# A recurrence stage with four rows to a partition: seven scan matmuls in place of ten, one queue for its transfers

## What is computed

```python
kv = ctx * ctx
r  = 0.9 * r + kv_t                 # row after row
x  = x + layernorm(x) * r           # first stage
h  = relu(quant_linear(layernorm(x), w1, b1))
x  = x + quant_linear(h, w2, b2)    # second and third stage
```

## Time and profile before

| | |
|---|---|
| median of 3 runs | 1264.55 us (1264.29 to 1264.74) |
| the profiled execution: its time | 1265.31 us |
| its span | 1263.5 us |
| mean granted clock of TensorE | 0.987 of full speed |
| TensorE matmuls busy | 1213.5 us, 96% |
| ScalarE busy | 979.9 us, 78% |
| VectorE busy | 872.2 us, 69% |
| GpSimd busy | 162.3 us, 13% |
| moved by DMA | 448.78 MB |

### The profile page before, as it was taken

One profiled execution on the slowest core, in us unless ns is written; L12 is line 12 of the kernel. 1 busy time (PEld: TensorE's weight loads), 2 busy tenths in 40 slices (PEclk: granted clock), 3 DMA queues, 4 the chain that ended last, 5 costly groups with the idle time before them and its releaser, 6 DMA issues.

```text
span 1263.5 us, 15533 instructions
## 1 busy us (share of the span) xinstructions
PE 1213.5 (96%) x5386; PEld 562.1 (44%) x5386; DVE 872.2 (69%) x1262; ACT 979.9 (78%) x1211; POOL 162.3 (13%) x394
## 2 busy tenths in 40 slices
PE   5998999999699999999999999799999999999997
PEld 2444444444344444444444444344444444444443
DVE  4887999886577777777777777566545655654554
ACT  4788999887577777777777776688887888888776
POOL 2646556444000000000000000000000000000000
PEclk9999999999799999999999999899999999999999
DMA  9999999972277799999999998699999999999998
GB/s 354 403 406 333 389 363 341 346 277 81 118 321 289 305 394 407 359 365 362 362 358 351 348 363 317 229 334 419 418 417 417 417 418 417 417 418 416 416 417 325
DMA packets 134614, 448.78 MB, mean 355 GB/s; under 512 B 10740, under 2 KB 10760, under 8 KB 123400
## 3 DMA queue, kind: packets, MB, share of 16 engines
q1 hardware_dynamic: 94744, 331.40, 66.2%
q10 hardware_dynamic: 39792, 116.40, 25.8%
HBM read 254.81 MB, written 192.94 MB: 354 GB/s over the span
## 4 chain that ended last, share of the span: by engine, by line
PE 80%; POOL 6%; issue 5%; DVE 4%; DMA 3%; ACT 2%; SPq 1%; ACTq 0%; POOLq 0%; DVEq 0%
PE ps L833 35%; PE ps L875 33%; PE ps L811 9%; PE ps L855 2%; DMA xq<-hidden_scratch 2%; POOL xq L444 2%; DVE st L644 1%; DVE st L630 1%; DVE xq L639 1%; DMA xq<-in_x_dram 1%; POOL rstd L436 1%; POOL cs_bc L428 1%; ACT xq L478 1%; ACT xq L589 0%; SPq L317 0%
## 5 line engine op out<-in xcount | busy, mean ns | idle before, releaser
L875 PE MATMUL ps<-w2T,xq 128*128 128x512 f16 x2048 | 446.4, 381 | 4.2 <-ACT xq L589 3.8
L833 PE MATMUL ps<-xq,w1T 128*128 128x512 f16 x2048 | 448.7, 380 | 1.4 <-DVE xq L710 1.4
L589 ACT ACTIVATE xq<-xq,hb,hs 128x512 f16<-128x512 f32 x494 | 357.3, 801 | 83.6 <-PE ps L875 57.5
L701 DVE TENSOR_REDUCE work<-xq 128x2 f32<-128x1024 f32 x255 | 311.0, 1220 | 125.9 <-ACT xq L534 125.9
L534 ACT ACTIVATE xq<-ps 128x1024 f32<-128x1024 f32 x255 | 260.9, 1023 | 123.1 <-PE ps L833 122.9
L875 PEld LDWEIGHTS ps<-w2T,xq 128*128 128x128 f16 x2048 | 200.0, 98 | 250.6 <-ACT xq L589 9.8
L811 PE MATMUL ps<-xq,work 128*128 128x512 f32 x640 | 283.0, 603 | 24.7 <-ACT xq L468 24.7
L833 PEld LDWEIGHTS ps<-xq,w1T 128*128 128x128 f16 x2048 | 199.1, 98 | 237.0 <-issue 1.9
L749 DVE TENSOR_TENSOR work<-ps,cs_bc 128x512 f32<-128x512 f32 x128 | 88.4, 691 | 185.0 <-PE ps L875 178.6
L811 PEld LDWEIGHTS ps<-xq,work 128*128 128x128 f32 x640 | 122.9, 193 | 178.0 <-issue 161.0
L478 ACT ACTIVATE xq<-ps,ones,cs_bc 128x512 f32<-128x512 f32 x128 | 98.9, 772 | 24.8 <-PE ps L811 23.8
(11 more groups left out here) (99 smaller groups left out, 444.9 us busy)
## 6 DMA issues: line engine op xcount, KB each, us to landing
hidden_scratch<-xq SPq DMA_DIRECT2D x240, 512.0 KB, 6.0
xq<-hidden_scratch SPq DMA_DIRECT2D x232, 512.0 KB, 21.2
work<-x_scratch ACTq DMA_DIRECT2D x42, 1024.0 KB, 11.4
xq<-in_ctx_dram ACTq DMA_DIRECT2D x31, 1024.0 KB, 9.2
xq<-in_x_dram SPq DMA_DIRECT2D x24, 1024.0 KB, 12.0
x_scratch<-xq SPq DMA_DIRECT2D x24, 1024.0 KB, 8.4
out_dram<-work ACTq DMA_DIRECT2D x24, 1024.0 KB, 12.0
xq<-in_L_ffn_w_dram SPq DMA_DIRECT2D x8, 1024.0 KB, 7.8
```

What stands on the lines that cost most here:

```text
L589: act.activation(hq[c % HQ], src[:, c % 2, :], ACT.Relu, bias=hb[:, q:q + 1], scale=hs[:, q:q + 1]).then_inc(h_scaled, 1)
L701: dve.tensor_reduce(hmax[:, b * NF + 2 * q:b * NF + 2 * q + 2], src, AX.X, ALU.max).then_inc(kept_maxed, 1)
L833: last = pe.matmul(bank, w1T[:, k, f * P:(f + 1) * P], xq_rows(b, k), start=(k == 0), stop=(k == KD - 1))
L875: last = pe.matmul(acc_bank(s, i), src[:, i * P:(i + 1) * P], w2T[:, q, :], start=first, stop=final)
```

## The change

- **Rows.** Partition p holds rows 4 p to 4 p + 3 of a batch; tile i holds rows 4 p + i. The three rearranges read `(p i)`; a partition's part of a batch is now 8 KB in one piece in DRAM, before four pieces of 2 KB.
- **Scan.** Tile 0 takes four matmuls over all four tiles of squares (`scan_first`). Tiles 1 to 3 each add one matmul on the same bank: the tile's own squares times a diagonal matrix with 0.9 to the power of -i (`scan_next`). The factor 0.9 to the power of i that this leaves out is put into the reciprocal deviation of x by three new constants (`half_x`, `per_row_x`, `eps_x`). That is seven matmuls a batch. The one bank of a batch is read by ScalarE between these steps, so `scan_next` waits until ScalarE has read the tile before.
- **Order.** Tiles of batch j and j + 1 are interleaved: (j+1, 0), (j, 2), (j+1, 1), (j, 3). A ring of four tiles holds the scaled sums, before eight. ScalarE squares batch j + 3 at the end of round j.
- **Rings.** CS is 4, statistics rings 8 batches, x statistics one batch further ahead (XLEAD = 4), LEAD 6.
- **Transfers.** SyncE issues all of the first stage: in each round the store of the finished batch, x, a weight quarter, ctx. The load of ctx waits for `scan_ready` of the batch whose buffer it takes.
- **Weights.** VectorE copies one of the two turned halves (`keep_weights`, 128x1024 float16), ScalarE the other.
- **End.** The y statistics of the last two batches are one group, before two.

```diff
-            ctx_rows = ctx_in.rearrange("b (i p) d -> b p i d", p=P)
+            ctx_rows = ctx_in.rearrange("b (p i) d -> b p i d", p=P)
...
+    for j in range(-1, NB):
+        scans += [t for t in ((j + 1, 1), (j, 3), (j + 1, 2), (j + 2, 0)) if 0 <= t[0] < NB]
+        tiles += [t for t in ((j + 1, 0), (j, 2), (j + 1, 1), (j, 3)) if 0 <= t[0] < NB]
...
+            def load_ctx(j):
+                if j >= CS:
+                    sp.wait_ge(scan_ready, scan_at[(j - CS, NI - 1)] + 1)
+                sp.dma_start(ct[j % CS], ctx_rows[j]).then_inc(ctx_loaded[j % CS], 16)
...
             for j in range(NB):
+                if j > 0 and j - 1 not in late:
+                    store_x2(j - 1)
                 if j + LEAD < NB:
                     load_x(j + LEAD)
                 for m in weights_at(j + 2):
                     if m > 0:
                         load_weights(m)
-                if j > 0 and j - 1 not in late:
-                    store_x2(j - 1)
+                if j + CS < NB:
+                    load_ctx(j + CS)
...
             def factors(j, i):
-                act.wait_ge(scan_ready, u + 1)
-                wait_count(act, x2_done, u + 1 - 2 * NI)
-                act.activation(g1[j % 2][:, i, :], scan_bank(j, i), ACT.Identity, bias=ones[:, 0:1],
+                act.wait_ge(scan_ready, scan_at[(j, i)] + 1)
+                wait_count(act, x2_done, n + 1 - len(g1))
+                act.activation(g1[n % len(g1)], scan_bank(j), ACT.Identity, bias=ones[:, 0:1],
...
+            x_stats_of(0)
+            x_stats_of(1)
+            product(0)
+            product(1)
+            y_stats(0)
+            x_stats_of(2)
+            x_stats_of(3)
+            for n in range(2, NU):
+                j, i = divmod(n - 2, NI)
+                product(n)
+                y_stats(n - 1)
+                if j < NB - 1:
+                    x_stats(j + XLEAD, i)
+                if i == NI - 1:
+                    for m in weights_at(j):
+                        weight_scales(m)
+                    for m in weights_at(j - 3):
+                        keep_weights(m)
...
-            def scan(j, i):
-                terms = [(k, kv[:, i - k, :]) for k in range(i + 1)]
-                for k, rows in terms:
-                    last = pe.matmul(bank, decay_mat[:, k * P:(k + 1) * P], rows, start=(k == 0), stop=(k == terms[-1][0]))
-                last.then_inc(scan_ready, 1)
+            for j in range(-1, NB):
+                scan_first(j + 2, 0)
+                scan_next(j + 1, 1)
+                scan_first(j + 2, 1)
+                scan_next(j, 3)
+                scan_first(j + 2, 2)
+                scan_next(j + 1, 2)
+                scan_first(j + 2, 3)
```

More of the change, by code:

```diff
@@ L36 @@
 XS = 11
-CS = 3
-RING = 4
+CS = 4
+RING = 8
+XLEAD = 4
 LATE = 6
-LEAD = 5
+LEAD = 6
 BIAS_AT = 21
@@ L86, in build @@
     quarters = [(w, k) for w in range(2) for k in range(4)]
+    scans, tiles = [(0, 0)], []
+    for j in range(-1, NB):
+        scans += [t for t in ((j + 1, 1), (j, 3), (j + 1, 2), (j + 2, 0)) if 0 <= t[0] < NB]
+        tiles += [t for t in ((j + 1, 0), (j, 2), (j + 1, 1), (j, 3)) if 0 <= t[0] < NB]
+    scan_at = {t: n for n, t in enumerate(scans)}
+    tile_at = {t: n for n, t in enumerate(tiles)}
     def weights_at(j):
@@ L393, in _ @@
             gp.wait_ge(gp_step, 1)
-            for m, w in ((impulse, 4 * P), (ident[:, :], P), (ident_b[:, :], P)):
+            for i in range(NI):
+                part = impulse[:, i * P:(i + 1) * P]
+                gp.affine_select(out=part, in_=part, compare_op=ALU.not_equal, fill=DECAY ** (NI - i) if i else 1.0, base=1 if i else 0,
+                                 pattern=[[-1, P]], channel_multiplier=1)
+            for i in range(1, NI):
+                gp.memset(decays[:, i * P:i * P + 1], 0.0)
+            for m in (ident[:, :], ident_b[:, :]):
                 last = gp.affine_select(out=m, in_=m, compare_op=ALU.not_equal, fill=1.0, base=0,
-                                        pattern=[[-1, w]], channel_multiplier=1)
+                                        pattern=[[-1, P]], channel_multiplier=1)
             last.then_inc(consts_ready, 1)
@@ L448, in _ @@
             x_stats(x_group[1])
-            for j in range(NB):
-                if j % 2 == 1 and j + 1 < NB:
-                    x_stats(x_group[j + 1])
-                if j % 2 == 0 and j >= 2:
-                    y_stats(y_group[j - 1])
+            x_stats(x_group[2])
+            for j in range(NB - 2):
+                if j % 2 == 1:
+                    if j + XLEAD < NB:
+                        x_stats(x_group[j + XLEAD])
+                    y_stats(y_group[j])
                 for m in weights_at(j):
                     round_weights(m)
-            y_stats(y_group[NB - 2])
             y_stats(y_group[NB - 1])
@@ L611, in _ @@
             link(dve.tensor_tensor_scan(decay_mat, decays, impulse, 0.0, ALU.mult, ALU.add))
+            for i in range(1, NI):
+                link(dve.tensor_scalar(own_mat[:, (i - 1) * P:i * P], ident[:, :], DECAY ** -i, None, ALU.mult))
             def weight_scales(m):
@@ L803, in turn_biases, with scan_first, scan_next @@
                 pe.transpose(ps[:, 7, NF:NF + KD], brow2[:, :], ident[0:KD, 0:KD]).then_inc(b_turned, 1)
[L805 to L818 removed]
+            def scan_first(j, k):
+                if not 0 <= j < NB:
+                    return
+                if k == 0:
+                    pe.wait_ge(ctx_squared, j + 1)
+                    if j >= 6:
+                        pe.wait_ge(scan_scaled, tile_at[(j - 6, NI - 1)] + 1)
+                last = pe.matmul(scan_bank(j), decay_mat[:, k * P:(k + 1) * P], ct[j % CS][:, k, :], start=(k == 0), stop=(k == NI - 1))
+                if k == NI - 1:
+                    last.then_inc(scan_ready, 1)
+            def scan_next(j, i):
+                if not 0 <= j < NB:
+                    return
+                pe.wait_ge(scan_scaled, tile_at[(j, i - 1)] + 1)
+                pe.matmul(scan_bank(j), own_mat[:, (i - 1) * P:i * P], ct[j % CS][:, i, :], start=False, stop=True, skip_group_check=True).then_inc(scan_ready, 1)
+            pe.wait_ge(dve_step, 1)
+            for k in range(NI):
+                scan_first(0, k)
+            pe.wait_ge(dve_step, NI)
+            for j in range(-1, NB):
[6 more added lines that the diff above has]
+                scan_first(j + 2, 3)
                 for m in weights_at(j - 2):
```

139 lines of the change are left out of this document (71 added, 68 removed).

## The result

The changed kernel takes 1242.9 us (median of 4 runs, 1240.6 to 1246.04) against 1264.43: a ratio of 0.9831, 95% interval 0.9805 to 0.9857. It is 21.5 us faster. The forecast was 1232.5, its range 1223 to 1253. The profiled execution took 1241.11 us with a span of 1239.2, 24.3 us less than the span before; the four runs spread over 5.4 us, those of the kernel before over 0.5.

What follows compares the result with a forecast made beforehand. TensorE was taken to bound the first stage's end, a mixture its part with weights, VectorE next. Gain 39 - 5 - 1 - 1 = 32 us: 1265.3 - 32 = 1233.3, against the median 1232.5 us; range 1223 to 1253.

Steps and rivals of the forecast that it cites:

- TensorE: First stage: 96 matmuls fewer, 82.5 us less work at most; 6.0 us a batch, below every other engine; busy near 200 us.
- The start: First batches: x of batch 3 usable at 22.2 us, VectorE's statistics done at about 24.6; nothing gained by batch 1.
- VectorE's work: First stage, the new bound: 265.6 us with 5.2 for eight copies, of which 254.2 are left from 24.6 us on.
- Its waits: VectorE in the first stage: 5 us given back for waits on ScalarE, bounds zero to 13; 1 us for the last tiles.
- Sum of the stage: First stage: 39 - 5 - 1 - 1 = 32 us gained, first `quantize` at 292 us (288 to 301).
- The later stages: Second and third stage: held at their old length, 939.3 us, since only the output's storage in 8 KB pieces touches them.
- The rest: Step from profiled execution to median: 0.8 us taken off, 1233.3 to 1232.5 us.
- SyncE's queue: First-stage transfers: ctx wanted 10 us after release; 5.2 us queued ahead and 2.6 of its own fit, 2 to spare.
- rival 1: First stage: transfers become the bound; at 344 GB/s 1264 us, chance 0.04; at 365 GB/s 1247 us, chance 0.10.
- Rival 2: Handshake of ScalarE and TensorE: at 0.3 us a tile, 11 us in batches without weights, 1244 us; chance 0.15.
- Rival 3: First stage: TensorE, idle more often, drops to its low clock, 12 us a batch, 1341 us; chance 0.07.
- ScalarE's burst: First stage: square, conversion and one copy, 4.8 us without a tile, fit under the four-tile ring's 7.2 us of VectorE.

Runs made afterwards that it cites:

- run 9: Changed kernel with three more matmuls on constants in every round, ten a batch as before: 1259.53 us, ratio 0.9952 to the kernel before.
- run 5: Changed kernel with, at the start alone, tile 1 of batch 0 added and scaled before batch 1 is touched: 1241.84 us, ratio 0.9825.
- run 6: Changed kernel with three filling matmuls ahead of every second batch of the part with weights: 1238.85 us, ratio 0.9792 to the kernel before.
- run 10: Changed kernel with both turned halves of a weight quarter copied by ScalarE again: 1251.95 us, ratio 0.9903 to the kernel before.
- run 3: Changed kernel with scans of tiles 1 to 3 in banks of their own, not waiting for ScalarE's tile (sum incomplete): 1236.38 us, ratio 0.9763.
- run 4: Changed kernel with ctx loads from batch 4 on issued by ScalarE on its own queue: 1247.06 us, ratio 0.9848 to the kernel before.
- run 7: Changed kernel with the store of the finished batch behind the ctx load in each SyncE round: 1245.21 us, ratio 0.9842.
- run 1: Kernel before with only its output rows laid out as in the change, 8 KB store pieces instead of 2 KB: 1268.05 us, ratio 1.0021.
- run 2: Changed kernel with each third-stage output store issued as two transfers, pieces of 2 KB again: 1240.36 us, ratio 0.9803 to the kernel before.

## Why the prediction was right or wrong

Right within its range, and 10 us too hopeful. Its mechanism held: TensorE's bound went, VectorE's came, and run 9 shows both sides. Its size came out near in part by luck, since VectorE's work was put 5.2 us too high and its waits 6.1 us too low. The stage ended as follows against my steps.

- **TensorE.** The 96 matmuls go, and the next engine takes over: right. The size is not: up to the first quantize TensorE is busy 234 us where it was 291, so 57 us less and not 82.5, and not "near 200". The passes that are left take 568 ns of busy time each in place of 442, mostly through the low clock: from 197 to 251 us, at the full one, it is about 450. Run 9 shows the hand-over; the 18 us that come back with three matmuls are the difference between two bounds and not the work removed.
- **The start.** I put the third product at 24.6 us; it came at 27.57. The transfers were in time: VectorE did the statistics of batches 2 and 3 without a wait. What I had left out is that the second product stands ahead of them in VectorE's order and came at 21.60, behind the square of batch 1 and TensorE's matmuls (the window of 10 to 20 us has a clock of 0.86). +3.0 us in this term; run 5 shows that an earlier second product does not bring the end of the stage forward.
- **VectorE's work.** From there 249.0 us against my 254.2: the copy was sized right, the collisions with GpSimd were fewer. -5.2 us.
- **Its waits.** 12.1 us against 5 and 1 for the last tiles. This is the step that was mis-sized: +6.1 us. I had named 13 as its outer bound. Where they lie is shown: 6.0 us in the part with weights, 2.3 from 197 to 251 us, 3.8 behind it. What makes them is shown only in part. In the part with weights runs 6 and 10 point at ScalarE's burst, the handshake and the low clock behind it, as one loop. From 197 to 251 us ScalarE waits for no scan but 2.7 us for ctx, and by runs 3, 4 and 7 the transfers stand right behind. The last 3.8 us, without full transfers, belong to the last tiles, for which I had given 1. After the last statistics it is 7.14 us to the quantize, 0.3 less than I had.
- **Sum of the stage.** 3.0 - 5.2 + 6.1 - 0.3 = 3.6 us later than forecast, 295.8 and not 292.3.
- **The later stages.** "I hold both at their old length" failed: +4.0 us in the third, of which about 2 are the larger pieces of the output (runs 1 and 2). I had read the third stage as TensorE's from 449 of 460 us and passed over the DMA share of 0.99 in the same row.
- **The rest.** The forecast took 0.8 us off, since the profiled execution of the kernel before was slower than its median. Beside the changed kernel's runs that is 0.9 us, and the changed kernel's own profiled execution was 1.8 us faster than its median, so a difference of 24.2 us between the profiled executions is one of 21.5 us between the medians. The scatter was not explained.
- **SyncE's queue.** The sum that ended with "it fits with 2 us to spare" failed: in the changed kernel ScalarE waits for ctx eight times, 7.0 us in all, between 25 and 300 us. By the prediction's own signs this was rival 1 showing itself.
- **Rival 1.** From 197 to 251 us transfers ran at 404 GB/s in the changed kernel and at up to 413 in run 3, with a share of 1.00, so rival 1's 344 and 365 did not come. The Trainium skill, "DMA: Bandwidth & Descriptors", section "Where 436 GB/s comes from", has the HBM's share of a core, about 358 GB/s, bind such transfers; these rates lie above it, so that rule did not decide here. But my check of 102.8 MB at 404 GB/s was a check of the end only. Inside the stage the demand after the weights is 3.15 MB in 7.2 us, 437 GB/s, more than any stretch of the first stage moved in any window read here. Three of the seven rounds after batch 18 still took 7.2 us; their mean became 7.67. This term was in my rows and I did not divide it out.
- **Rival 2.** I had named the batches without weights as its place and 11 us as its price. There, from 197 to 251 us at the full clock, ScalarE waits for no scan; it waits where the clock is low, in the part with weights. All that run 3 gains in the stage by leaving the handshake out is 3.4 us, 1.8 of it between batches 18 and 25, where no such wait explains it.
- **Rival 3.** The clock did fall, to 0.87 in the mean of the part with weights, each time behind an idle stretch of 2.05 to 2.96 us in which ScalarE squares, converts and copies; TensorE had nearly 3 us a batch to spare there (9.3 less 6.0 and half of 1.06 us of turning), so it cost a few us and not 77. The Trainium skill's warning, "TensorE: Matmul & The Clock Gate", section "A second HAM failure mode: psum-queue depth-cycling", blames short idles between groups of matmuls that cycle through banks. The trace does not bear this out: from 197 to 251 us the short waits are there (TensorE waits ten times, 6.0 us in all), and the clock is 1.00.
- **ScalarE's burst.** "It fits" was nearly right at 4.8 us with four tiles of cover: VectorE waits 0.4 to 0.9 us behind six of the eight weight rounds. Run 10 shows that 1 us more is 10 us later. I charged the split of the copies as a cost and did not see what it buys.

## What to carry to other kernels

When three engines stand at 94, 86 and 84% and the transfers near a full share, relieving the first gives the distance to all the others together: set the demand of the new round (bytes over the new round's time, the longest burst against the buffer that covers it) against what each can give, and not only the sums of work. An engine that is made less busy can become slower: here TensorE's granted clock went from 0.99 to 0.87 in the part with weights, and a few filling matmuls in the idle places brought it back to 0.97. They are worth a try. A layout that is changed for one stage changes the transfers of every stage that shares it: here it cost about 2 us in the third stage, which the change was not meant to touch.

## What the hardware showed that I had not expected

- Adding 27 matmuls to TensorE's queue in the idle places raised the granted clock from 0.84 to 0.97 (80 to 140 us), and the kernel was not slower for it (ratio 0.9792 against 0.9831, with intervals that touch).
- With 30% of the scan matmuls gone, the busy time of the scans fell by 10% only, from 283.0 to 254.6 us, since the passes that are left ran in part at the low clock.
- Pieces of 8 KB in place of 2 KB loaded 407 and 428 GB/s where 387 were moved (10 to 30 us), and stores of 1 MB landed in 7.9 us where they had taken 12.0, without making the kernel before faster; for the output stores they made it 2.7 us slower.
- Two queues for the same loads brought nothing: in run 4 ctx was still waited for, 8.1 us against 7.0, and the DMA moved 386 GB/s against 389 from 48 to 197 us.
